# Batch 1's normalised rows in a fused attention and MLP block: scaled on VectorE and turned by DMA in groups 2 and 3

## The reference

```
mod = swish(c) @ w_mod + b_mod
sh_msa, sc_msa, g_msa, sh_mlp, sc_mlp, g_mlp = split(mod, 6, axis=1)
xn = _ln(x) * (1 + sc_msa[:, None, :]) + sh_msa[:, None, :]
q, k, v = heads(xn @ w_qkv + b_qkv)          # 16 heads of 36
q, k = _ln(q, g_q), _ln(k, g_k)
attn = softmax(q k^T * 36 ** -0.5)
x = x + g_msa * ((attn v) @ w_proj + b_proj)
x = x + g_mlp * (gelu(( _ln(x) * (1 + sc_mlp) + sh_mlp) @ w1 + b1) @ w2 + b2)
```

## Time and profile before

| | |
|---|---|
| three runs | 2806.61, 2806.68, 2809.34 us; median 2806.68 |
| the profiled execution | 2808.21 us, its span 2806.4 us |
| granted TensorE clock, mean | 0.995 of full speed |
| TensorE, busy | 2751.7 us, 98% of the span |
| VectorE, busy | 1991.5 us, 71% |
| ScalarE, busy | 1516.2 us, 54% |
| GpSimd, busy | 677.6 us, 24% |
| chain of waits that ended last | TensorE 91%, VectorE 4%, all others 1% or less each |

### The profile page before, as it was taken

The page is one execution under the profiler, slowest core; times in us unless marked ns, Lnnn a source line. Parts: engine busy times, 40 slices in busy tenths (PEclk is TensorE's granted clock), DMA queues, the critical chain, the costliest instruction groups (busy, mean ns, idle before and its releaser), DMA issues.

```text
span 2806.4 us, 42780 instructions
## 1 busy us (share of the span) xinstructions
PE 2751.7 (98%) x14754; PEld 1415.7 (50%) x14754; DVE 1991.5 (71%) x2689; ACT 1516.2 (54%) x2222; POOL 677.6 (24%) x522
## 2 busy tenths in 40 slices
PE   6899999999999999999999999999999999999999
PEld 3444444444444444444444444447566575756656
DVE  7799999888888888888898899952534344353421
ACT  4677777788877777777777777621211212111110
POOL 2543344322233333333343322300000000000000
PEclk9999999999999999999999999999999999999999
DMA  7412322222211122222223233041120202112000
GB/s 221 89 30 69 96 74 74 75 53 53 53 30 30 30 71 62 74 68 72 71 73 80 51 113 120 21 148 40 51 68 23 90 10 82 43 49 73 19 18 18
DMA packets 238609, 181.28 MB, mean 65 GB/s; under 512 B 151511, under 2 KB 187805, under 8 KB 237765
## 3 DMA queue, kind: packets, MB, share of 16 engines
q1 hardware_dynamic: 238182, 179.31, 23.4%
q10 hardware_dynamic: 288, 0.04, 0.0%
HBM read 99.70 MB, written 46.04 MB: 52 GB/s over the span
## 4 chain that ended last, share of the span: by engine, by line
PE 91%; DVE 4%; ACT 1%; POOL 1%; issue 1%; DMA 1%; SPq 1%; ACTq 0%; DVEq 0%
PE at_ps L1708 19%; PE at_ps L1075 15%; PE at_ps L1072 15%; PE at_ps L1063 15%; PE at_ps L1734 15%; PE at_ps L1093 10%; DVE at_plo L865 2%; PE at_ps L1727 1%; PE at_ps L1128 1%; PE at_ps L1672 1%; PE at_ps L1689 1%; ACT at_p L681 0%; POOL at_ssq L568 0%; PE at_ps L1104 0%; DVE at_wq L268 0%
## 5 line engine op out<-in xcount | busy, mean ns | idle before, releaser
L865 DVE TENSOR_TENSOR at_plo<-at_p 128x1024 fp32r<-128x1024 f32 x1024 | 1269.5, 1260 | 185.9 <-ACT at_p L681 182.3
L681 ACT ACTIVATE at_p<-at_ps 128x1024 f32<-128x1024 f32 x1024 | 1047.7, 1026 | 413.6 <-PE at_ps L1063 413.0
L1075 PE MATMUL at_ps<-at_plo,at_vr 128*37 128x512 f32 x2048 | 1074.4, 592 | 0.0
L1072 PE MATMUL at_ps<-at_p,at_v 128*73 128x512 bf16 x2048 | 797.8, 390 | 6.3 <-DVE at_plo L865 6.2
L1708 PE MATMUL at_ps<-ml_w2s,ml_hid 128*128 128x288 f16 x3456 | 429.8, 287 | 2.0 <-issue 2.0
L1708 PEld LDWEIGHTS at_ps<-ml_w2s,ml_hid 128*128 128x128 f16 x3456 | 338.8, 98 | 87.8 <-issue 2.5
L1734 PE MATMUL at_ps<-ml_xhi,ml_w 128*128 128x512 f16 x1296 | 381.9, 379 | 0.0
L1072 PEld LDWEIGHTS at_ps<-at_p,at_v 128*73 128x73 f16 x2048 | 233.1, 114 | 250.7 <-DVE at_plo L865 11.5
L552 POOL TENSOR_TENSOR at_tssq<-at_tssq,head_eps 128x8 f32<-128x8 f32 x112 | 123.9, 1106 | 965.6 <-DVE at_tssq L826 965.6
L1075 PEld LDWEIGHTS at_ps<-at_plo,at_vr 128*37 128x37 f32 x2048 | 233.9, 114 | 222.4 <-issue 1.5
L1063 PE MATMUL at_ps<-at_qk_even 109*128 (+1 forms) x1024 | 310.5, 385 | 7.7 <-DMA at_qk_even<-at_stk 4.0
(11 more groups left out here) (178 smaller groups left out, 2284.3 us busy)
## 6 DMA issues: line engine op xcount, KB each, us to landing
head_sums<-at_oT SPq DMA_DIRECT2D x256, 72.0 KB
ml_held<-head_sums SPq DMA_DIRECT2D x64, 256.0 KB
at_xy<-in_L_cond_w SPq DMA_DIRECT2D x34, 288.0 KB
w_halves<-at_wq SPq DMA_DIRECT2D x68, 144.0 KB
at_xy<-in_x SPq DMA_DIRECT2D x32, 288.0 KB, 2.9
ml_x<-in_x SPq DMA_DIRECT2D x8, 1152.0 KB, 5.4
out<-ml_x SPq DMA_DIRECT2D x7, 1152.0 KB, 4.5
ml_held<-head_rden SPq DMA_DIRECT2D x24, 216.0 KB
```

The costliest lines, as they stand in the source:

```text
L681: act.activation(p[:, s % NP, :], ps[:, 2 * (s % 2):2 * (s % 2) + 2, :].rearrange("p a n -> p (a n)"), ACT.Exp).then_inc(exp_done, 1)
L865: nc.vector.tensor_tensor(plo[:, s % NP, :], p[:, s % NP, :], high, ALU.subtract).then_inc(plo_ready, 1)
L1072: nc.tensor.matmul(acc[0:VW, bass.ds((U % 2) * CH, CH)], v16[:, h % 2, 2 * s + a, 0:VW], high, start=(s == 0 and a == 0), stop=False, skip ...
L1075: last = nc.tensor.matmul(acc[0:RW, bass.ds((U % 2) * CH, CH)], vr[:, h % 2, 2 * s + a, 0:RW], plo[:, s % NP, a * CH:(a + 1) * CH], start= ...
```

## The change

Batch 1's rows are no longer normalised in group 1, stored and turned in group 2. Instead 16 tiles of rows are done in one pass, 11 in units 0 to 10 of group 2 and 5 in units 0 to 4 of group 3. Each has these stages:
- SyncE loads the tile's rows once the low part of the tile before is done.
- VectorE subtracts the mean and multiplies by (1 + scale) in step 1, and multiplies by the reciprocal deviation and adds the shift in step 2. Both are `scalar_tensor_tensor` on 128 x 576 float32, in place.
- ScalarE casts 576 columns to float16 in step 4 and repeats the last 64.
- VectorE subtracts to get the low part in step 5.
- SyncE turns high and low part by two DMA transposes of 128 x 640 float16, straight into `xhi` and `xlo`.

The parts, and the scale and shift rows spread over all partitions (590 KB), lie in the columns of `qkT[(G + 1) % 2]` that the group's last units fill. So SyncE loads the rows at the start of each of the two groups, once the scores that read this buffer are issued; GpSimd then adds 1 to the scale and fills a strip of the low part with ones, and VectorE's first scaling waits for both. In the start phase SyncE stores the two vectors of batch 1 to DRAM. TensorE's transposes, ScalarE's scalings and `y_dram` are gone. VectorE's units of groups 2 and 3 are written out instead of looped, and ScalarE's loops of these groups are split in two. The reciprocal deviations are still made at the start of group 1. The diff, cut to what is spoken of here:

```diff
+    def store_mods(self, sp, mods_dram):
+        sp.wait_ge(self.rows_taken, 1)
+        for n, q in ((0, 32), (1, 0)):
+            sp.dma_start(mods_dram[n:n + 1, :], self.rows[0][q + 16:q + 17, 0:H]).then_inc(self.mods_stored, 16)
...
-        STATS_IN, Y_IN, HATS_IN = NG - 4, NG - 3, NG - 2
+        STATS_IN, RSTD_IN, HATS_IN = NG - 4, NG - 3, NG - 2
+        HATS = 11
+        HOLE = HATS * P
+        SCALED_AT, SHIFTED_AT, HAT_HIGH_AT, HAT_LOW_AT = 1, 2, 4, 5
...
+        hat_hi, hat_lo = ([qkT[(G + 1) % 2][:, e, HOLE:N] for G in (HATS_IN, HATS_IN + 1)] for e in range(2))
+        scale_row, shift_row = ([t[:, e:e + 2, HOLE // 2:HOLE // 2 + HALF] for t in (start.later[HATS_IN % 2], start.later[1 - HATS_IN % 2])] for e in (2, 4))
+        halved = lambda ap: ap.rearrange("p (a n) -> p a n", a=2)
...
+        def hat_of(G, u):
+
+            if G == HATS_IN and (not isinstance(u, int) or u < HATS):
+                return u
+            if G == HATS_IN + 1 and (not isinstance(u, int) or u < NT - HATS):
+                return u + HATS
+            return None
...
+            start.store_mods(sp, mods_dram)
...
+            sp.wait_ge(start.mods_stored, 16 * 2)
...
-                if G == Y_IN:
+                r = hat_of(G, u)
+                if r is not None:
                     if u == 0:
-                        sp.wait_ge(n_mv, NT + 1)
-                    sp.wait_ge(n_stored, 16 * u + 16)
-                    sp.dma_start(xy[:, 0:H], xf[bass.ds(N + u * P, P), :]).then_inc(n_loaded, 16)
-                if G == HATS_IN:
-                    if u == 0:
-                        sp.wait_ge(n_stored, 16 * NT + 16)
-                    sp.wait_ge(n_lo, u + 1)
-                    sp.dma_start(xy[:, :], y_dram[bass.ds(u * P, P), :]).then_inc(ny_loaded, 16)
+                        sp.wait_ge(scores_ready, G * UNITS * STEPS)
+                        both = start.later[G % 2][:, 2:6, HOLE // 2:HOLE // 2 + HALF]
+                        sp.dma_start(both, bcast(mods_dram.rearrange("v (a n) -> (v a) n", a=2), 0, P)).then_inc(n_rows, 16)
+                    sp.wait_ge(n_lo, r + 1)
+                    sp.dma_start(xy[:, 0:H], xf[N + r * P:N + r * P + P, :]).then_inc(n_loaded, 16)
                 i = U - SLICED * UNITS
                 if 0 <= i < SLICES:
...
+                    if G in (HATS_IN, HATS_IN + 1) and u == HATS:
+                        sp.wait_ge(n_turned, 32 * (HATS if G == HATS_IN else NT) + 32)
...
-                if G == Y_IN:
-                    sp.wait_ge(n_whole, u + 1)
-                    sp.dma_start(y_dram[bass.ds(u * P, P), :], xy[:, :]).then_inc(n_stored, 16)
+                if r is not None:
+                    sp.wait_ge(n_lo, r + 2)
+                    for part, whole in ((hat_hi, xhi), (hat_lo, xlo)):
+                        sp.dma_start_transpose(whole[:, :, r * P:(r + 1) * P], part[G - HATS_IN]).then_inc(n_turned, 16)
...
-                if U == Y_IN * UNITS:
+                if U == RSTD_IN * UNITS:
...
+                if u == 0 and hat_of(G, u) is not None:
+                    n = G - HATS_IN
+                    pool.wait_ge(n_rows, 16 * (n + 1))
+                    pool.tensor_scalar(scale_row[n], scale_row[n], 1.0, None, ALU.add)
+                    pool.memset(hat_lo[n][:, H:KC * P], 1.0).then_inc(n_hole, 1)
...
-            def hats(u, ks):
-                col = lambda v, k: keep.cols[:, 1, v, k:k + 1]
-                for k in ks:
-                    act.wait_ge(n_turned, 2 * u + (1 if k < KF else 2))
-                    act.activation(xy[:, k * P:(k + 1) * P], hat_bank[:, (k % KF) * P:(k % KF + 1) * P], ACT.Identity,
-                                   bias=col(0, k), scale=col(1, k)).then_inc(n_aff, 1)
-
-            def hats_high(u):
-                act.wait_ge(n_aff, (u + 1) * KC)
-                act.copy(xhi[:, :, bass.ds(u * P, P)], xy[:, :].rearrange("p (k n) -> p k n", k=KC)).then_inc(n_hi, 1)
+            def hat_high(n, r):
+                act.wait_ge(n_hat, r + 1)
+                act.wait_ge(n_turned, 32 * r + 32)
+                act.copy(hat_hi[n][:, 0:H], xy[:, 0:H])
+                act.copy(hat_hi[n][:, H:KC * P], xy[:, KF * P:H]).then_inc(n_hi, 1)
...
-                    if G == HATS_IN and s == 5:
-                        hats(u, range(KF))
-                    if G == HATS_IN and s == 7:
-                        hats(u, (KF,))
-                        hats_high(u)
+                    if hat is not None and s == HAT_HIGH_AT:
+                        hat_high(G - HATS_IN, hat)
...
+                elif G in (HATS_IN, HATS_IN + 1):
+                    done = HATS if G == HATS_IN else NT - HATS
+                    with act.Fori(0, done) as u:
+                        unit(G, u, hat=hat_of(G, u))
+                    with act.Fori(done, UNITS - 1) as u:
+                        unit(G, u)
...
+            def hat_scaled(n, r):
+                if isinstance(r, int) and r in (0, HATS):
+                    dve.wait_ge(n_hole, n + 1)
+                    dve.wait_ge(n_rstd, 1)
+                dve.wait_ge(n_loaded, 16 * (NT + r + 1))
+                nc.vector.scalar_tensor_tensor(out=halved(xy[:, 0:H]), in0=halved(xy[:, 0:H]), scalar=nmv[:, r, 0:1], in1=scale_row[n],
+                                               op0=ALU.subtract, op1=ALU.mult).then_inc(n_scaled, 1)
+
+            def hat_shifted(n, r):
+                dve.wait_ge(n_scaled, r + 1)
+                nc.vector.scalar_tensor_tensor(out=halved(xy[:, 0:H]), in0=halved(xy[:, 0:H]), scalar=nrstd[:, 1, r:r + 1], in1=shift_row[n],
+                                               op0=ALU.mult, op1=ALU.add).then_inc(n_hat, 1)
+
+            def hat_lower(n, r):
+                dve.wait_ge(n_hi, r + 1)
+                nc.vector.tensor_tensor(hat_lo[n][:, 0:H], xy[:, 0:H], hat_hi[n][:, 0:H], ALU.subtract).then_inc(n_lo, 1)
+
...
-                    if G == Y_IN and s == 6:
-                        if isinstance(u, int) and u == 0:
-                            dve.wait_ge(n_rstd, 1)
-                        dve.wait_ge(n_loaded, 16 * (NT + u + 1))
-                        nc.vector.tensor_scalar(xy[:, 0:H], xy[:, 0:H], nmv[:, u, 0:1], nrstd[:, 1, u:u + 1], ALU.subtract, ALU.mult).then_inc(n_y, 1)
-                    if G == Y_IN and s == 7:
-                        dve.wait_ge(n_y, u + 1)
-                        nc.vector.tensor_copy(xy[:, H:KC * P], xy[:, KF * P:H]).then_inc(n_whole, 1)
-                    if G == HATS_IN and s == 7:
-                        tok = bass.ds(u * P, P)
-                        dve.wait_ge(n_hi, u + 1)
-                        nc.vector.tensor_tensor(xlo[:, 0:KF, tok], xy[:, 0:KF * P].rearrange("p (k n) -> p k n", k=KF), xhi[:, 0:KF, tok], ALU.subtract)
-                        nc.vector.tensor_tensor(xlo[0:KT, KF, tok], xy[0:KT, KF * P:], xhi[0:KT, KF, tok], ALU.subtract).then_inc(n_lo, 1)
+                    if hat is not None and s == SCALED_AT:
+                        hat_scaled(G - HATS_IN, hat)
+                    if hat is not None and s == SHIFTED_AT:
+                        hat_shifted(G - HATS_IN, hat)
+                    if hat is not None and s == HAT_LOW_AT:
+                        hat_lower(G - HATS_IN, hat)
...
-                if G in (STATS_IN, Y_IN, GROUPS - 1):
+                if G <= HATS_IN + 1 or G == GROUPS - 1:
...
-                        pe.wait_ge(n_lo, t + 2)
+                        pe.wait_ge(n_turned, 32 * t + 64)
...
-            def hat_turns(u, ks):
-
-                pe.wait_ge(ny_loaded, 16 * u + 16)
-                if KF in ks:
-                    pe.wait_ge(n_aff, u * KC + KF)
-                for k in ks:
-                    last = nc.tensor.transpose(hat_bank[:, (k % KF) * P:(k % KF + 1) * P], xy[:, k * P:(k + 1) * P], keep.ident[:, :])
-                last.then_inc(n_turned, 1)
...
-                    if G == HATS_IN and s == 4:
-                        hat_turns(u, range(KF))
-                    if G == HATS_IN and s == 7:
-                        hat_turns(u, (KF,))
...
-                        if G == HATS_IN + 1:
-                            pe.wait_ge(n_aff, NT * KC)
...
-    y_dram = nc.dram_tensor("normal_rows", (N, KC * P), F32, kind="Internal").ap()
+    mods_dram = nc.dram_tensor("mod_rows", (2, H), F32, kind="Internal").ap()
```

More of the change, by code:

```diff
@@ L90, in __init__ @@
         self.tails, self.bias_hi = xhi[:, 0, N - CH:N - CH + self.COLS], xhi[:, 1, N - CH:N - CH + self.COLS]
-        later = [sb(f"later{g}", [P, QK, N // 2], F32, at) for g, at in ((2, 126720), (3, 75520))]
+        later = self.later = [sb(f"later{g}", [P, QK, N // 2], F32, at) for g, at in ((2, 126720), (3, 75520))]
         self.word = [[t[:, i, N // 4:N // 4 + self.COLS] for i in range(self.SLICED)] for t in later]
@@ L330, in split_products, with attention_mlp @@
         yield xlo[:, KF, tokens], w[:, 8, cols]
-def attention_mlp(nc, keep, place, x, c, w_mod, b_mod, w_qkv, b_qkv, g_q, g_k, b2, sums_dram, den_dram, rden_dram, y_dram, out, halves,
```

(12 more changed lines are left out.)

14 lines of the change are left out of this document (7 added, 7 removed).

## The result

| | before | after | forecast |
|---|---|---|---|
| median of the runs, us | 2806.72 (4 runs) | 2827.09 (4 runs, 2825.57 to 2830.65) | 2797.4 |
| ratio to before, 95% interval | | 1.0070 (1.0058 to 1.0081) | 0.997 |
| profiled execution: time, span | 2808.21, 2806.4 | 2828.42, 2826.6 | 2798.9 |
| group 1, first copy to first copy | 217.78 | 216.43 | 216.6 |
| group 2 | 228.73 | 237.86 | 218.8 |

The kernel became 20.4 us slower, and the forecast said 9.3 us faster. The forecast of a group is its own time of before with the terms that the prediction gave it. The range ended at 2805.5: the sign was wrong.

A forecast was written before the change was run, and what follows sets the result against it. TensorE, busy in 98% of the span, was taken to bound the kernel. The terms -13.3 - 1.2 + 2.2 + 2.0 + 1.0 gave -9.3 us, thus 2797.4 us against the median, range 2792 to 2805.5.

The forecast's parts named there:

- What goes in groups 2 and 1: Groups 2 and 1: removing batch 1's turning and normalising saves 13.3 us in group 2 and 1.2 us in group 1.
- An undisturbed unit: Unit with a row, away from head work: VectorE's added operations cost about 0.2 us of waiting, 2.2 us over 11 units.
- Units behind head work: Units 3 and 7 of group 2, unit 3 of group 3: scaling delays step 2, 0.65 us each, 2.0 us.
- Unit 0: Start of groups 2 and 3: broadcast load of 2.9 to 5.4 us makes scaling late, 1.0 us (0 to 4).
- The queues: SyncE's queue: the row load and two transposes are in time, the row covered by 0.9 us; cost nothing.
- Rival D: SyncE's queue, low part to next scaling: row comes late, 2808 or 2834 us; chance 0.15, half of it slower.
- Rival C: GpSimd's power gets in only behind the new low part, L830 0.5 us later, 7.7 us more, 2805.1; chance 0.13.
- the slower side: Whole kernel measured above 2812.3 us: chance 0.07, the hard half of Rival D.

The follow-up runs named there:

- experiment 9: Changed kernel plus a one-column VectorE memset behind step 4's subtraction in the 16 units with a row, timed in five rounds: 2798.65 us, ratio 0.9974 to the kernel before.
- experiment 2: Changed kernel with the scaling and shift operations of steps 1 and 2 each replaced by a one-column memset: 2796.32 us.
- experiments 7: Changed kernel plus a one-column VectorE memset behind step 4's subtraction in units with a row, one profiled run: 2799.09 us.
- experiment 1: Changed kernel with the low part of the rows moved from step 5 to step 6, behind the head normalisation: 2839.19 us.
- experiment 8: Changed kernel with GpSimd's epsilon addition moved to VectorE in all groups, GpSimd keeping the power: 2810.94 us.
- experiment 11: Changed kernel plus two unused two-input VectorE operations in steps 1 and 2 of groups 4 and 5, group 5 also with the memset: 2840.72 us.

## Why the prediction was wrong

- **What goes in groups 2 and 1: right.** With the losses taken out (experiment 9), group 2 is 9.5 us and group 1 1.35 us shorter than before; forecast were 9.9 and 1.2.
- **An undisturbed unit: right in its sum.** In experiment 9 it takes 13.67 to 13.84 us, mostly 13.69, against 13.66. The split is less sure: without scaling and shift (experiment 2) most units of group 2 still take 13.62 to 13.64. So of the 0.2 us over 13.46 the two operations account for some 0.05, where the sum had 0.17 for the shift, and the casts and the low part for the rest. Scaling and shift last 0.81 us, not the 0.75 assumed. That the sum met the time so closely is in part luck.
- **Units behind head work: right in size, once nothing is lost (experiments 7 and 9).** 14.27, 14.25 and 14.17 in experiment 9, against 14.1. They have the longest lag there, 1.18 to 1.28 us.
- **Unit 0: right, a little high.** 13.69 and 13.77 in experiment 9, against 13.96. The broadcast landed in 4.7 us, inside the bounds.
- **The queues: right.** Rival D didn't come. The row's load is issued at 617.22 in the good unit and at 630.89 in the hit one, 3.35 us behind the start of the low part in both, with a median of 3.0 us to landing, and the scaling never waits for it. Only in experiment 1, with the low part a step later, did it wait.
- **Rival C: the right place, the wrong instruction and price.** It had the lock move GpSimd's *power*, behind *one* operation, at 0.48 us a unit. What is moved is the addition before it, behind up to *three* more operations, at 1.9 us of TensorE's time, and 1.7 more where the clock falls. Groups 2 and 3 together are 465.3 us with the losses and 436.7 without (experiment 9), 28.6 us more: eight units at about 3.55 us and one at 1.9 are 30, less what a unit behind a hit catches up (unit 3 takes 13.57 us in both groups, 14.27 and 14.17 in experiment 9).
- **The step that failed** is the sentence in C, "The rows say that it slips in at the end of whichever operation runs", by which the sum put L830's wait for GpSimd at nothing. What happened instead: nine additions waited through four operations, 4.05 us instead of 1.11, and L830 then waited 1.8 us for the power in each of these units. The rows shown are of an unhurried VectorE: the lag there is 903.43 - 903.10 = 0.33 us. The change makes the lag grow, to 0.57 us and more, and I carried the rule over to a state that those rows don't show. I also looked only at the power, since it is the longer of the two. The trace of before held the counterexample, in a word unit of group 1 behind head work (timeline of VectorE and GpSimd):

```profile
432.03 2.34 DVE L865 TENSOR_TENSOR at_plo<-at_p 128x1024 fp32r<-128x1024 f32 x2
432.19 2.25 POOL L552 TENSOR_TENSOR at_tssq<-at_tssq,head_eps 128x8 f32<-128x8 f32 x1 [4.23 <-DVE at_tssq L826]
434.41 0.60 DVE L268 SCALAR_TENSOR_TENSOR at_wq<-st_later 1x432 f16<-1x432 f32 x1
```

One addition in 112 took 2.25 us instead of 1.11, at a lag of 0.82 us. It waited through two subtractions, up to an operation on a single partition. The mean of the group, 1106 ns, hides it; the longest one would have shown it. With it, C would have had to price an addition that waits for the whole row up to L830, and the slower side would have had a chance worth naming.
- **TensorE's clock** had no term either. It fell behind eight of the nine waits and makes up about 13 of the 28 us.

The forecast's price of the work itself comes out: 2797.4 us against the 2798.65 of experiment 9, which has the memset besides. For the change as it was made the forecast was wrong.

## What to carry to other kernels

When a change fills VectorE ahead of a deadline, count not only the microseconds: a short GpSimd instruction on the path that reads SBUF may have got in only because VectorE kept close to its producer. Look for the longest, not the mean, of each small instruction on the path. Where operations with two SBUF inputs stood back to back here, a memset of one column between them, 0.06 us long, was worth 28 us. It belongs right behind the operation during which the GpSimd instruction is released; one operation later it was worth only three quarters (2805.63 against 2798.65 and 2827.09). Try it and measure: the power of experiment 8 needed none.

## What the runs showed of the hardware

- The Trainium skill, page "SBUF — State Buffer", section "Who interferes with whom", says that a VectorE instruction with two SBUF inputs contends with a GpSimd instruction that reads SBUF. The runs agree and add that the waiting side isn't always served at the end of the operation that runs: an addition of eight columns waited through four VectorE operations, 4.05 us. At a lag of 0.33 us the same addition was served behind the first of them, in 1.11 us, and so was the power at a lag of 1.34 us.
- TensorE's clock: beside 1.93 us of idling the granted clock fell to 0.50 for 3.4 us in one unit, and it stayed 1.00 after the same 1.93 us in the next. Over all kernels 35 of the 52 additions of over 3 us went with such a fall and 17 did not. The length of the wait alone doesn't tell: in experiment 11 TensorE idled 2.53 us before 601.32 and kept 1.00. I had not counted a clock cost for waits this short. Here it nearly doubled them.
